# A three-layer compressed interaction network in float32: each tile's x and its layer 1 operand brought in by one transfer over 128 partitions, in place of four over 32 partitions

## What is computed

```python
h = x0
for i in range(3):
    H = h.shape[1]                      # 32, then 64, 64
    Wk = Ws[i].reshape(128, H, 32)
    xk = relu(einsum('bhd,bmd,ohm->bod', h, x0, Wk) + bs[i][None, :, None])
    if i != 2:
        outs.append(xk[:, :64]); h = xk[:, 64:]
    else:
        outs.append(xk)
return concatenate([o.sum(axis=-1) for o in outs], axis=1)     # 512 x 256
```

## Time and profile before

| | |
|---|---|
| time, median of 3 runs | 1851.83 us (1851.81 to 1856.69) |
| the profiled execution's own time | 1852.14 us |
| its span | 1850.4 us |
| PE busy | 1799.8 us, 97% of the span |
| DVE busy | 1551.5 us, 84% |
| POOL busy | 1468.2 us, 79% |
| ACT busy | 1095.6 us, 59% |
| read from HBM | 153.75 MB |
| transfers of X / of XD / of the hidden state | 256 of 512 KB / 256 of 64 KB / 640 of 64 or 128 KB |

### The profile page before, as it was taken

One profiled execution on the slowest core, in us unless ns is written; L12 is line 12 of the kernel. 1 busy time (PEld: TensorE's weight loads), 2 busy tenths in 40 slices (PEclk: granted clock), 3 DMA queues, 4 the chain that ended last, 5 costly groups with the idle time before them and its releaser, 6 DMA issues.

```text
span 1850.4 us, 18060 instructions
## 1 busy us (share of the span) xinstructions
PE 1799.8 (97%) x6284; PEld 1184.2 (64%) x6284; DVE 1551.5 (84%) x850; ACT 1095.6 (59%) x899; POOL 1468.2 (79%) x324
## 2 busy tenths in 40 slices
PE   3899999999999999999999999999999999999997
PEld 1566666666666666666666666666666666666665
DVE  3998898898888888888888888888888888988974
ACT  2566656656656666566565665665666666566562
POOL 0788878878878778778778778778778788788786
PEclk9999999999999999999999999999999999999998
DMA  8455455455454454454454454554554553553510
GB/s 203 107 125 128 92 123 121 96 126 117 97 128 111 101 129 107 104 128 108 103 129 107 106 128 101 113 128 98 116 128 96 118 128 88 126 127 88 127 26 20
DMA packets 62169, 205.83 MB, mean 111 GB/s; under 512 B 18816, under 2 KB 19968, under 8 KB 53888
## 3 DMA queue, kind: packets, MB, share of 16 engines
q1 hardware_dynamic: 62080, 204.68, 49.5%
HBM read 153.75 MB, written 0.52 MB: 83 GB/s over the span
## 4 chain that ended last, share of the span: by engine, by line
PE 96%; POOL 1%; DMA 1%; SPq 1%; ACT 1%; DVE 0%; issue 0%; DVEq 0%; POOLq 0%; ACTq 0%
PE ACC L384 24%; PE ACC L400 19%; PE ACC L394 19%; PE ACC L397 19%; PE ACC L375 12%; PE ACC L378 3%; POOL ZL L291 1%; DMA ZS<-in_w 1%; ACT ZH L313 0%; DVE ZS L221 0%; SPq L159 0%; DVE ZW L204 0%; ACT HP L306 0%; DMA H<-H 0%; SPq L140 0%
## 5 line engine op out<-in xcount | busy, mean ns | idle before, releaser
L291 POOL TENSOR_TENSOR ZL<-ZS,ZH 128x2048 fp32r<-128x2048 f32 x320 | 1468.0, 4616 | 373.2 <-ACT ZH L313 373.2
L313 ACT ACTIVATE ZH<-ZS 128x2048 fp32r<-128x2048 f32 x384 | 734.2, 1912 | 536.7 <-PE ACC L400 415.0
L221 DVE TENSOR_TENSOR ZS<-HP,X 128x2048 f32<-128x2048 f32 x384 | 870.5, 2281 | 151.4 <-ACT HP L306 150.1
L394 PE MATMUL ACC<-ZH,WL 128*128 128x512 f32 x1536 | 497.6, 446 | 7.7 <-ACT ZH L313 7.7
L384 PE MATMUL ACC<-ZW,WF 128*128 128x512 f32 x1024 | 460.3, 592 | 0.0
L400 PE MATMUL ACC<-ZL,WH 128*128 128x512 f32 x1536 | 421.7, 396 | 8.4 <-POOL ZL L291 8.3
L397 PE MATMUL ACC<-ZH,WH 128*128 128x512 f32 x1536 | 421.0, 396 | 0.0
L394 PEld LDWEIGHTS ACC<-ZH,WL 128*128 128x128 f32 x1536 | 289.6, 189 | 152.3 <-issue 99.3
L216 DVE TENSOR_TENSOR ZW<-HP,X 128x2048 f32<-128x2048 f32 x128 | 292.2, 2283 | 101.3 <-PE ACC L384 101.3
L400 PEld LDWEIGHTS ACC<-ZL,WH 128*128 128x128 f32 x1536 | 287.8, 188 | 81.5 <-POOL ZL L291 11.5
L397 PEld LDWEIGHTS ACC<-ZH,WH 128*128 128x128 f32 x1536 | 288.8, 188 | 70.3
(11 more groups left out here) (32 smaller groups left out, 164.5 us busy)
## 6 DMA issues: line engine op xcount, KB each, us to landing
X<-in_xpad SPq DMA_DIRECT2D x256, 512.0 KB, 8.4
H<-H SPq DMA_DIRECT2D x512, 64.0 KB, 2.0
XD<-in_xpad SPq DMA_DIRECT2D x256, 64.0 KB, 2.0
H<-H SPq DMA_DIRECT2D x128, 128.0 KB, 2.2
ZS<-in_w SPq DMA_DIRECT2D x6, 256.0 KB, 10.3
WF<-in_w SPq DMA_DIRECT2D x2, 256.0 KB, 11.1
out<-XD SPq DMA_DIRECT2D x4, 128.0 KB, 1.8
W<-in_w SPq DMA_DIRECT2D x1, 320.0 KB, 3.0
```

Of the source, the lines that this page charges most:

```text
L221: nc.vector.tensor_tensor(ZS[:, n % SSLOTS, :, :], h, x, ALU.mult).then_inc(prod_ready, 1)
L291: nc.gpsimd.tensor_tensor(ZL[:, n % SSLOTS, :, :], ZS[:, n % SSLOTS, :, :], ZH[:, n % SSLOTS, :, :], ALU.subtract).then_inc(low_by_pool, 1)
L313: nc.scalar.activation(ZH[:, n % SSLOTS, :, :], ZS[:, n % SSLOTS, :, :], ACT.Copy).then_inc(high_ready, 1)
L394: nc.tensor.matmul(ACC[layer][:, :], wl[:, g, :], ZH[:, n % SSLOTS, g, :], start=(k == 0 and g == 0), stop=False)
```

## The change

The host lays x out twice. `xrows` has ROWS = 136 rows per tile, ordered so that partition p's eight rows are rows p to p+7 of it, and one transfer over 128 partitions (row pitch 2 KB, 16 KB each) fills a slot of X. `xdup` is x four times over, so that one transfer fills XD. The semaphores count 16 in place of 64 per load. For some partitions the eight rows of x are other ones than before, and `shift_rows` gives the weights the same order. All sizes in SBUF, all instructions of PE, DVE, ACT and POOL and the bytes of each load are what they were.

```diff
+ROWS = 128 + XC
...
+def x_rows():
+
+    n = np.arange(ROWS)
+    return (n % BLK + XC * (n // BLK)) % M
...
 def shift_rows():
 
-    p = np.arange(128)
-    s = np.arange(XC)[None, :] + XC * (p // BLK)[:, None]
-    return (p % BLK)[:, None], ((p % BLK)[:, None] + s) % M
+    p = np.arange(128)[:, None]
+    return p % BLK, x_rows()[p + np.arange(XC)[None, :]]
...
             def load_x(t):
                 slot = t % XSLOTS
-                for k in range(NB):
-                    src = bass.AP(xpad.tensor, (t * 2 * M + XC * k) * T, [[T, BLK], [1, XC * T]])
-                    to = X[BLK * k:BLK * k + BLK, slot, :, :].rearrange("p j t -> p (j t)")
-                    sp.dma_start(to, src).then_inc(x_loaded[slot], 16)
+                src = bass.AP(xrows.tensor, t * ROWS * T, [[T, 128], [1, XC * T]])
+                sp.dma_start(X[:, slot, :, :].rearrange("p j t -> p (j t)"), src).then_inc(x_loaded[slot], 16)
 
             def load_xd(t):
-                for k in range(NB):
-                    src = bass.AP(xpad.tensor, t * 2 * M * T, [[T, BLK], [1, T]])
-                    sp.dma_start(XD[BLK * k:BLK * k + BLK, t % 2, :], src).then_inc(xd_loaded[t % 2], 16)
+                sp.dma_start(XD[:, t % 2, :], xdup[t, :, :]).then_inc(xd_loaded[t % 2], 16)
...
-                dve.wait_ge(x_loaded[i % XSLOTS], 16 * NB * (i // XSLOTS + 1))
+                dve.wait_ge(x_loaded[i % XSLOTS], 16 * (i // XSLOTS + 1))
...
-                act.wait_ge(xd_loaded[t % 2], 16 * NB * (t // 2 + 1))
+                act.wait_ge(xd_loaded[t % 2], 16 * (t // 2 + 1))
...
-    xpad = np.concatenate([x, x], axis=1)
+    xdup = np.concatenate([x] * NB, axis=1)
...
-        "xpad": xpad, "w1": w1, "w1t": w1t,
+        "xrows": x[:, x_rows()], "xdup": xdup, "w1": w1, "w1t": w1t,
```

More of the change, by code:

```diff
@@ L52, in lows_before, with cin_kernel @@
     return sum((u in BY_DVE) == by_dve for u in order[:n])
-def cin_kernel(nc, xpad, w1, w1t, w2, w3, bias, ident_in, out):
+def cin_kernel(nc, xrows, xdup, w1, w1t, w2, w3, bias, ident_in, out):
     f32, f32r = mybir.dt.float32, mybir.dt.float32r
```

## The result

| | before | after |
|---|---|---|
| median, us | 1852.03 (19 runs) | 1848.21 (19 runs, 1847.25 to 1849.69) |
| ratio to before | | 0.9977, 95% interval 0.9971 to 0.9984 |
| the profiled execution's own time, us | 1852.14 | 1848.21 |
| its span, us | 1850.4 | 1846.4 |

The change takes 3.8 us off, a clear gain that is smaller than 0.3%. The time lies in the stated range, 1.9 us above the forecast of 1846.3.

A forecast was written before the change was run, and what follows sets the result against it. PE was taken to bound the kernel, busy 1799.8 of 1850.4 us, with idle time mainly at the start. 1852.14 less 5.85 for faster first loads, other terms 0, gave 1846.3 us; own range 1844.0 to 1848.6, with rivals to 1850.4.

The forecast's parts named there:

- The bound and the steady state: From 76 to 1830 us PE runs without a gap, so faster loads of x save nothing there.
- Issues priced at nothing: At the start, six fewer issues send the weights some 2.4 us earlier, but they only wait longer in the queue: 0.
- The cause of the rate: Loads of X and XD at the start: 32 partitions against 128 set 208 GB/s; the change would give 389.
- The rival of a reader's limit: Load of X: reading overlapping 16 KB rows sets the rate, so the transfer gets no faster; 1852.1 us, chance 0.07.
- The slower rival: Load of X: 128 streams hinder each other at HBM, the rate falls to 137 GB/s; 1863.3 us, chance 0.05.
- The term of 5.85 us: At the start, the 2.78 MB of 4 to 17 us take 7.15 us at 389 GB/s in place of 13.
- The prediction's own sign of being wrong: At the start: w3 lands later than 18 us; other signs were slow matmuls in unbroken work or waits in the middle.
- PE's clock: At the first product, its eight matmuls may see more or less low clock: up to 2.3 us either way.
- The term of the first split product: After a longer PE pause it may meet the low clock, hidden by waits for POOL: taken at 0.
- the rival with only part of the rate: Load of X keeps a limit of its own at 291 GB/s: 3.4 us saved, 1848.7 us, chance 0.10.
- The second tile's wait for X goes, worth nothing: At the start, DVE's 3.98 us wait for tile 1's X goes, but is not on the chain: no gain.

The follow-up runs named there:

- all but tile 0: Changed kernel, but tile 0's X and XD by four transfers over 32 partitions each, tiles 1 to 63 by one over 128: 1852.14 us.
- the comb: Changed kernel, but X of a tile by four transfers over 32 partitions each, every fourth one: 1847.72 us, ratio 0.9975 to the kernel before.
- the blocks: Changed kernel, but X of a tile by four transfers over 32 neighbouring partitions each, from the new array: 1852.91 us, ratio 1.0003 to the kernel before.
- the halves: Changed kernel, but X of a tile by two transfers over 64 neighbouring partitions each: 1853.72 us, ratio 1.0007 to the kernel before.
- the copy moved and the old loads: Kernel before the change, with ACT's copy of XD of tile 0 moved ahead of rounding w2 and w3: 1848.68 us, ratio 0.9980.
- the five rows first: Changed kernel with XD of tile 0 copied early, and its X in two transfers, layer 1's five rows first: 1839.57 us, ratio 0.9933.

## Why the prediction was right or wrong

**The bound and the steady state: right.** The middle did not change, and the 63 other tiles' loads are worth nothing (all but tile 0: ratio 1.0000).

**Issues priced at nothing: right.** They shrank by 2.8 us at the start and a version with three of them back is as fast.

**The cause of the rate: right**, by the comb, the blocks and the halves, but for the stretch of HBM, which went along with the partitions. The rival of a reader's limit falls in the form that was given: overlapping rows of 16 KB are read at up to 410 GB/s. The slower rival falls with it. One argument for the cause was weak: the dip to 137 GB/s was put down to DMA engines that a transfer can't use, but their share is 0.81 there, and near 1 for the whole slow load.

**The term of 5.85 us: too large.** The first product came 5.17 us earlier in the profiled execution. "At 389 GB/s they take 7.15 us" fails from 4 to 6 us, where the rate was 219; from 6 to 16 us the mean is 385, about what was taken. X of tile 0 landed at 12.0 us, not before 11. And this was a fortunate execution. The instants at which ACT began to round w3, in all profiles:

| tile 0's X by | executions | w3 rounded from, us | rate from 6 to 12 us, GB/s |
|---|---|---|---|
| blocks of 32 or 64 | 5 | 21.61 to 23.05, mean 22.1 | 213 to 232 |
| transfers spread over 128 | 9 | 16.97 to 19.30, mean 18.2 | 333 to 394 |

By the means the term is 3.9 us, not 5.85, and 3.9 is nearly all of the 3.8 between the medians. The prediction's own sign of being wrong, w3 later than 18 us, was absent in the profile of the changed kernel (16.95) and is there in six of these nine executions. Two kernels with the same transfers up to w3 (the change, and the one with 14 idle matmuls) differ by 2.3 us here. In the latter the rate was 143 GB/s from 4 to 6 us, in others up to 310. These 2 us don't tell the landing by themselves: with 310 GB/s in them w3 was rounded from 18.71, with 160 from 17.81. What holds the DMA engines up in some executions stays open.

**PE's clock: the sign of the first products was left open, and it went against.** From the start of the first product to relu it took 24.20 to 34.63, 10.4 us, before, and 19.03 to 30.34, 11.3 us, now: 0.9 us back, within the 2.3 either way. It is the difference of two single executions: in the eleven profiles without idle matmuls the eight take 5.31 to 6.43 us with the slow loads (five) and 5.65 to 6.64 with the fast ones (six), so it isn't shown that the change brings it. The term of the first split product was taken at 0 and was 0: the low clock came as said, and POOL hid it. Not in my sum was the drain, where the clock rises a little later (four matmuls at 1831.96 take 1.58 us, where 1836.24 had 1.18): the last matmuls start 3.92 us earlier (1847.09 to 1843.17), while the drain's first starts 4.28 us earlier (1828.03 to 1823.75), 0.36 us back.

**The account of the two profiled executions:** 5.85 expected, less 0.68 (rate), less 0.89 (first products), less 0.36 (drain) is 3.92, and its own time fell by 1852.14 - 1848.21 = 3.93 us.

**The range held in part by luck.** Its 2.3 us on the slow side were given for the clock of the first products alone. The miss of 1.9 us is made of the rate, that clock and the drain, and by the means of the loads (3.9 in place of 5.85) it is nearly all a matter of the loads. 1848.21 is in fact nearer to 1848.7, the time of the rival with only part of the rate, than to the forecast. The mean rate from 4 to 17 us, 362 GB/s in this profile and 334 to 364 in all nine, lies between the 389 of the one and the 291 of the other. What speaks for the forecast is that X has no such limit of its own: it came at up to 410.

**"The second tile's wait for X goes, worth nothing": right here**, and only here. With the copy moved and the old loads, and with the five rows first, that same landing set the chain.

## What to carry to other kernels

Let each transfer into SBUF write partitions that are spread over all 128; how many transfers there are matters far less, and here a comb of every fourth partition did as well as one large transfer. Price such a gain only where someone waits: here one tile's load of 64. Then look at what the waiter truly needs, since moving one copy ahead of two that wait for later data was worth twice the change.

## What was not expected of the hardware

- Transfers over 32 partitions each can take 401 to 404 GB/s, if they are every fourth one (four such transfers, issued one behind the other).
- With the same transfers ahead of it, w3 was in at times 2.3 us apart (16.97 and 19.30 us), and no row shows what held them up. One profile is a poor measure of a term of that size at the start.
- Idle matmuls help only if the pause behind them is short: after 3.02 us of pause the low clock was back (5.37 us for eight matmuls), after 2.20 and 0.29 us it was not (3.67 us each).
- The granted clock reads 1.00 in PE's first microseconds (third number from the right, changed kernel), while the eight matmuls take 6.60 us, 1.8 times the 3.67 us that they take behind 16 idle ones. That the low clock makes them slow is thus read from their times and not from the clock's row.

```profile
24.00:26.00 2.00, 2.00 (x4) 0.79 (x3) 1.97 (x2) 0.00 (x0) 0.00 (x0) 1.00 0.00 0
```
